# Expert rows loaded in blocks of 32 by 32 and turned by VectorE instead of TensorE

## The chip, the cores and the metric

The kernel runs on one core of one Trainium2 chip. The metric is device time in microseconds (us) of one launch; lower is better. Everything computes in f32 apart from routing masks and a few bf16 helpers.

## What is computed

The input has 32 sequences of 256 tokens with 128 channels (8192 tokens). There are two layers. Each normalises its input, computes an attention `s` and a mixture of experts `g`, and adds `s * silu(g)` to the input:

```python
xn = layernorm(x);  x = x + attention0(xn) * silu(moe0(xn))   # layer 0
xn = layernorm(x);  x = x + attention1(xn) * silu(moe1(xn))   # layer 1
# moe0: sigmoid gate, the best 2 of 8 experts, every token served; plus a shared expert
# moe1: softmax gate, the best 2 of 8 experts, at most 2048 places for each expert
# expert e: act(rows @ up_w[e] + up_b[e]) @ down_w[e] + down_b[e],  128 -> 512 -> 128
```

## The kernel before

The program is written out by hand for each engine, in the order in which the engine is to do things; semaphores order the engines among each other.

**Stages.** Routing decides for every token two places in a table of rows in HBM (`xd0`, `xd1`, one row of 132 floats for a place: 128 channels, and in word 128 the row of the result table to which the expert's output goes). POOL scatters the normalised rows there with indirect DMAs. When all are there, the experts run over **tiles** of 256 places: 71 tiles in layer 0 (`x0`) and 64 in layer 1 (`x1`). In layer 0 this stage stands between the first attention and the shared expert; in layer 1 it is put into the second attention, after its sequence 21.

**One tile.** In the text, tile i of a layer takes these steps:

- SP loads the 256 rows with one DMA into one of 6 buffers `X` (L453, two rows of 132 floats on each of 128 partitions). In layer 0, SP also loads each tile's expert weights: it reads the expert's number into a register (L437), then loads `up_w` (L438), `down_w` (L439) and the bias `down_b` (L441) into one of 5 buffers; layer 1 keeps an expert's weights for eight tiles and nearly all of them are loaded by ACT's queue.
- TensorE turns the two blocks of 128 rows with transposes into PSUM (`turn`, L1830), since the matmuls contract over channels and need them on the partitions.
- VectorE copies the turned rows to `XG` in SBUF (L1427), and computes the row numbers of the results, `to` (L1431).
- TensorE multiplies by `up_w` (`up`, L1839, four products of 256 columns), ScalarE applies bias and activation into `HH` (L874), and TensorE multiplies by `down_w` (`down`, L1848, 8 products).
- VectorE adds `down_b` (L1439, `result`), and POOL scatters the 256 result rows with two indirect DMAs (L622).

**Order.** TensorE goes turn(i+1), up(i), down(i-1), so a tile costs it the three steps. VectorE goes turned(i+1), result(i-1). SP goes, for each tile, rows of tile i+5, then the weights of tile i+4. Rows may be loaded into a buffer once `turn` and `to` of the tile before in it are done; weights once `edown` and `y` (down and result) of the tile before in their buffer are done:

```python
for i in range(x.n):                      # expert_rows, on SP
    if i + 5 < x.n:
        load(i + 5)
    if n == 0 and 1 <= i < x.n - 4:
        expert_weights(e, m, s, i + 4)
```

Tiles 0 to 3 of the rows and tiles 0 to 4 of the weights are loaded ahead of the stage. At its start in layer 0, SP waits for the end of the first attention (`yt`), loads constants and five blocks of the input (L528 to L532, L490), and then goes on with the rows of tile 4.

In layer 1 the first tiles stand around a piece of the second attention: TensorE does turn(0), up(0), then `output_second` of sequence 21, then turn(1) and turn(2).

Of the kernel before, what the change touches and what calls it, by code (L numbers as in the profile page):

```python
# [8 lines left out]
ALU = mybir.AluOpType  # L9
# [154 lines left out]
def memory(nc, ctx, a, out):  # L164
    m = Mem()

    def sbx(stack, name, shape, dt=F32):
        return stack.enter_context(nc.sbuf_tensor("s_" + name, shape, dt))
# [95 lines left out]
    es = ExitStack()  # L264
    m.DBt = [sbx(es, f"DBt{k}", [P, C]) for k in range(5)]
    x = m.x0 = Mem()
    x.n, x.base, x.NWB, x.NXB = NX0, 0, 5, 6
    x.W = [sbx(es, f"W0_{k}", [P, 2, 512]) for k in range(5)]
    x.X = [sbx(es, f"X0_{k}", [P, 2, ROW]) for k in range(6)]
    x.XG = [sbx(es, f"XG0_{k}", [P, SL]) for k in range(2)]  # L270
    x.HH = [sbx(es, f"HH0_{k}", [P, 4, SL]) for k in range(2)]
    x.Y = [sbx(es, f"Y0_{k}", [P, 2, C]) for k in range(4)]
    x.xr = m.xd0[0:NX0 * SL, :].rearrange("(i t p) c -> i p t c", p=P, t=2)
    x.yd = m.yd0
    m.H = [sbx(es, f"H{k}", [P, 4, 512]) for k in range(2)]
    m.swu = sbx(es, "swu", [P, HID])
# [37 lines left out]
    bt = ExitStack()  # L314
# [27 lines left out]
    x = m.x1 = Mem()  # L342
    x.n, x.base, x.NWB, x.NXB = NX1, NX0, 2, 6
    x.W = [sbx(bt, f"W1_{k}", [P, 2, 512]) for k in range(2)]
    x.X = [sbx(bt, f"X1_{k}", [P, 2, ROW]) for k in range(6)]
    m.b1s, m.b2s = sbx(bt, "b1s", [P, E, 4]), sbx(bt, "b2s", [P, E, C])
    bt.close()

# [15 lines left out]
    x = m.x1  # L364
    x.XG = [carve([SL]) for k in range(2)]
    x.HH = [carve([4, SL]) for k in range(2)]
    x.Y = [carve([2, C]) for k in range(4)]
    x.xr = m.xd1[0:NX1 * SL, :].rearrange("(i t p) c -> i p t c", p=P, t=2)
    x.yd = m.yd1
    carve = carver()  # L370
    m.ZG = [carve([8 * C]).rearrange("p (c k n) -> p c k n", c=4, k=2) for k in range(NF)]
# [6 lines left out]
def semaphores(nc, ctx):  # L378
    s = Sems()

    def sem(name):
        return ctx.enter_context(nc.semaphore(name))

    s.v_seq = sem("v_seq")

    s.const, s.upb, s.sw, s.zero, s.w0, s.c1, s.bb = (sem("l_" + n) for n in ("const", "upb", "sw", "zero", "w0", "c1", "bb"))
    s.zero_y, s.placed, s.to, s.nb, s.norm_a, s.norm_p, s.cnt_row = (sem(n) for n in (
        "l_zero_y", "placed", "to", "nb", "norm_a", "norm_p", "cnt_row"))

    s.wv0, s.vl, s.va, s.vd = (sem(n) for n in ("l_wv0", "vl", "va", "vd"))  # L390
    s.x = [sem(f"l_x{k}") for k in range(8)]
    s.scat0, s.scat1 = sem("l_scat0"), sem("l_scat1")

    s.zero_ready, s.var, s.rstd, s.norm, s.xpose, s.xt = (sem(n) for n in (
        "zero_ready", "var", "rstd", "norm", "xpose", "xt"))

    s.gate, s.gate_exp, s.onehot, s.cnt, s.cnt_sb, s.rank, s.total, s.total_sb, s.low, s.low_used, s.slots, s.ub = (
        sem(n) for n in ("gate", "gate_exp", "onehot", "cnt", "cnt_sb", "rank", "total", "total_sb", "low", "low_used",
                         "slots", "ub"))

    s.zvm, s.proj, s.rt, s.rq, s.ka, s.qm, s.vm, s.sc1, s.ev1, s.mask, s.sc2, s.prod, s.pv, s.yt = (sem(n) for n in (
        "zvm", "proj", "rt", "rq", "ka", "qm", "vm", "sc1", "ev1", "mask", "sc2", "prod", "pv", "yt"))

    s.turn, s.xg, s.eup, s.eact, s.edown, s.y = (sem(n) for n in ("turn", "xg", "eup", "eact", "edown", "y"))
    s.W = [[sem(f"l_W{n}_{k}") for k in range((5, 2)[n])] for n in range(2)]
    s.X = [[sem(f"l_X{n}_{k}") for k in range(6)] for n in range(2)]
    s.Y = [[sem(f"l_Y{n}_{k}") for k in range(4)] for n in range(2)]

    s.sup, s.hact, s.sdown = (sem(n) for n in ("sup", "hact", "sdown"))
    s.xb = [sem(f"l_xb{k}") for k in range(5)]  # L410
    s.yg = [sem(f"l_yg{k}") for k in range(3)]
    s.x1d = [sem(f"l_x1d{k}") for k in range(5)]
    s.comb, s.u, s.tanh, s.oproj, s.p6, s.x1, s.lg1, s.lg_sb = (sem(n) for n in (
        "comb", "u", "tanh", "oproj", "p6", "x1", "lg1", "lg_sb"))
# [30 lines left out]
def expert_rows(e, m, s, x, n):  # L445
    X, Y = s.X[n], s.Y[n]

    def load(i):
        k = i - x.NXB
        if k >= 0:  # L450
            e.wait_ge(s.turn, x.base + k + 1)
            e.wait_ge(s.to, x.base + k + 1)
        e.dma_start(x.X[i % x.NXB][:], x.xr[i]).then_inc(X[i % x.NXB], 16)  # L453

    for i in range(4):
        load(i)
# [8 lines left out]
    for k in range(4):  # L465
        e.wait_ge(Y[k], 32 * len(range(k, x.n, 4)))
# [952 lines left out]
def expert_dve(e, m, s, x, n, bias):  # L1419
    if n == 1:  # L1420
        e.wait_ge(s.bb, 32)

    def turned(i):
        e.wait_ge(s.turn, x.base + i + 1)
        if x.base + i >= 2:
            e.wait_ge(s.eup, 4 * (x.base + i - 1))
        e.tensor_copy(x.XG[i % 2][:], m.PS[6 + (i + n) % 2][:, 0:SL]).then_inc(s.xg, 1)  # L1427
        e.wait_ge(s.X[n][i % x.NXB], 16 * (i // x.NXB + 1))
        if i >= 8:
            e.wait_ge(s.Y[n][i % 4], 32 * (i // 4 - 1))  # L1430
# [12 lines left out]
    if n == 1:
        divide_second(e, m, s, MOE_AFTER)
        keep_second(e, m, s, MOE_AFTER)
    for i in range(x.n):
        if i + 1 < x.n:
            turned(i + 1)
        if i >= 1:
            result(i - 1)  # L1450
    if n == 1:
        maxima_dve(e, m, s, MOE_AFTER + 2, 0)
    result(x.n - 1)
# [360 lines left out]
def expert_pe(e, m, s, x, n):  # L1814
    PS = m.PS
# [6 lines left out]
        e.wait_ge(s.W[1][k % 2], 32 * (k // 2 + 1))  # L1822
        return x.W[k % 2]

    def turn(i):
        e.wait_ge(s.X[n][i % x.NXB], 16 * (i // x.NXB + 1))
        if x.base + i >= 2:
            e.wait_ge(s.xg, x.base + i - 1)
        for t in range(2):
            ins = e.transpose(PS[6 + (i + n) % 2][:, t * P:(t + 1) * P], x.X[i % x.NXB][:, t, 0:C], m.ident[:])  # L1830
        ins.then_inc(s.turn, 1)

    def up(i):
        W = weights(i)
        e.wait_ge(s.xg, x.base + i + 1)
        for j in range(4):
            if x.base + i >= 1:
                e.wait_ge(s.eact, 4 * (x.base + i - 1) + j + 1)
            e.matmul(PS[j][:, 0:SL], W[:, 0, j * P:(j + 1) * P], x.XG[i % 2][:], start=True, stop=True).then_inc(s.eup, 1)  # L1839
# [9 lines left out]
                               W[:, 1, j * C:(j + 1) * C], start=(j == 0), stop=(j == 3))  # L1849
        ins.then_inc(s.edown, 1)  # L1850

    turn(0)
    for i in range(x.n):
        if n == 1 and i == 0:
            up(0)
            output_second(e, m, s, MOE_AFTER)
            e.wait_ge(s.given, MOE_AFTER + 1)
            turn(1)
            continue
        if i + 1 < x.n:  # L1860
            turn(i + 1)
        up(i)
        if i >= 1:
            down(i - 1)
    if n == 1:
# [56 lines left out]
def tensor_program(e, m, s):  # L1922
    PS = m.PS
# [21 lines left out]
    for u in range(-1, NU + 4):  # L1945
        v, b = u % 6, u // 6
# [21 lines left out]
                route_ranks(e, m, s, m.r0, 0, stage - 2)  # L1968
        if v == 4 and b + 2 < NB:
            projection(e, m, s, b + 2, 0)  # L1970
    e.wait_ge(s.yt, NB)
    expert_pe(e, m, s, m.x0, 0)

    e.wait_ge(s.sw, 80)
    shared_up(e, m, s, 0)
    for g in range(NG):
# [25 lines left out]
    for t in range(NB + 1):  # L2002
# [42 lines left out]
        if t == MOE_AFTER:  # L2045
            weigh(e, m, s, t, 1)
            e.wait_ge(s.maxv, 4 * t + 8)
            e.wait_ge(s.ex, 4 * t + 4)
            e.wait_ge(s.mvt, t + 2)
            e.wait_ge(s.qs, t + 4)  # L2050
            expert_pe(e, m, s, m.x1, 1)


# [113 lines left out]
```

## Time and profile before

| | |
|---|---|
| median of 3 runs | 1727.6 us (1726.49 to 1728.92) |
| span of the profiled execution, first to last instruction | 1723.8 us |
| TensorE busy, share of the span | 95% |
| VectorE, ScalarE, POOL busy | 57%, 57%, 48% |
| mean granted TensorE clock | 0.994 of full speed |
| DMA traffic | 170.05 MB in 172423 packets, mean 99 GB/s |
| layer 0's experts on TensorE | from 527.15 to about 793.5 us |
| layer 1's experts on TensorE | from 1323.62 to about 1567 us |

No time of its own is given for the profiled execution beyond its span; the span is 3.8 us under the median of the runs, which takes in what lies around the first and the last instruction. Matmuls are pipelined, so their busy times overlap and the distance between starts tells what a step costs.

### The profile page before, as it was taken

The numbers are of one execution on the slowest core, as the hardware profiler recorded it, in microseconds if no ns is written. First come the engines' busy times: TensorE is split into PE (matmuls) and PEld (weight loads), VectorE is DVE, ScalarE is ACT, GpSimd is POOL, SyncE is SP. The second block draws the span as 40 slices with busy tenths as digits, with TensorE's granted clock in tenths as the row PEclk, the third lists the DMA queues.
The fourth block names the chain that finished last, engine by engine and source line by source line (L and its number), as shares of the span: only waits on it lengthen the run. The fifth ranks groups of instructions, "written<-read, shape, count | busy, mean of one in ns | idle before, by whom it ended". The sixth has DMA issues, their size and how long they took to land.

```text
span 1723.8 us, 49824 instructions
## 1 busy us (share of the span) xinstructions
PE 1629.9 (95%) x19349; PEld 1175.9 (68%) x19353; DVE 986.2 (57%) x2085; ACT 987.3 (57%) x2039; POOL 828.9 (48%) x906
## 2 busy tenths in 40 slices
PE   7999999999999999999998899898988999999995
PEld 5545454555547999998777566565656999997664
DVE  6788898777772222223999676454544222224887
ACT  5667666667664444444555465555555444445773
POOL 7343687877773454552122102555553555553323
PEclk9999999999999999999999899999999999999999
DMA  9900003000016777873342100111112223322434
GB/s 312 416 18 2 16 28 98 28 28 28 30 37 178 234 231 229 234 230 100 110 134 80 52 3 14 36 36 35 36 34 55 83 86 95 86 74 75 125 101 118
DMA packets 172423, 170.05 MB, mean 99 GB/s; under 512 B 20800, under 2 KB 139584, under 8 KB 169248
## 3 DMA queue, kind: packets, MB, share of 16 engines
q1 hardware_dynamic: 152768, 128.84, 24.9%
q0 software_dynamic: 16832, 34.64, 5.9%
q10 hardware_dynamic: 2592, 3.38, 0.7%
q8 instruction: 158, 2.59, 0.6%
q14 instruction: 73, 0.60, 0.1%
HBM read 97.16 MB, written 69.63 MB: 97 GB/s over the span
## 4 chain that ended last, share of the span: by engine, by line
PE 76%; DVE 7%; issue 5%; POOL 4%; another core or an unknown queue 3%; ACT 3%; DMA 1%; SPq 0%; POOLq 0%; DVEq 0%; ACTq 0%
PE ps L1848 14%; PE ps L1839 13%; PE ps L1641 10%; PE ps L1665 4%; PE ps L1605 4%; PE ps L1887 3%; PE ps L1875 3%; PE ps L1732 3%; PE ps L1798 3%; PE ps L1769 3%; PE ps L1606 2%; PE ps L1802 2%; PE ps L1779 2%; DVE s_RS L1318 2%
## 5 line engine op out<-in xcount | busy, mean ns | idle before, releaser
L605 POOL DMA_INDIRECT xd<-s_XN,s_slots x256 | 251.1, 981 | 143.8 <-issue 78.1
L793 ACT ACTIVATE s_S<-ps 128x512 f32<-128x512 f32 x384 | 209.9, 595 | 146.5 <-PE ps L1641 133.6
L1495 DVE TENSOR_TENSOR s_PP<-ps,s_S 128x1024 f32<-128x1024 f32 x192 | 234.4, 1221 | 85.4 <-PE ps L1641 52.8
L1641 PE MATMUL ps<-s_QM,s_KK 32*128 32x512 f32 x1536 | 241.6, 638 | 3.7 <-ACT s_S L793 3.6
L1318 DVE TENSOR_REDUCE s_RS<-ps 128x8 f32<-128x1024 f32 x128 | 150.7, 1218 | 160.6 <-PE ps L1736 85.3
L859 ACT ACTIVATE s_PX<-ps,s_scl 128x1024 f32<-128x1024 f32 x128 | 135.7, 1111 | 186.0 <-PE ps L1779 186.0
L622 POOL DMA_INDIRECT yd<-s_Y,s_to x142 | 136.1, 959 | 137.5 <-DVE s_to L1431 109.6
L874 ACT ACTIVATE s_HH<-ps,s_LG 128x256 f32<-128x256 f32 x284 | 123.6, 474 | 136.8 <-PE ps L1839 135.5
L638 POOL TENSOR_SCALAR_AFFINE_SELECT s_S<-s_S 128x1024 f32<-128x1024 f32 x128 | 140.7, 1099 | 120.8 <-ACT s_S L793 115.3
L874 ACT ACTIVATE s_XN<-ps,s_b1s 128x256 f32<-128x256 f32 x256 | 113.1, 474 | 126.3 <-PE ps L1839 120.2
L622 POOL DMA_INDIRECT yd<-s_XN,s_to x128 | 122.7, 958 | 129.8 <-DVE s_to L1431 102.6
L1439 DVE TENSOR_TENSOR s_Y<-ps,s_DBt 128x256 f32<-128x256 f32 x71 | 30.1, 425 | 199.5 <-PE ps L1848 188.3
L1848 PEld LDWEIGHTS ps<-s_W,s_HH 128*128 128x128 f32 x1136 | 137.8, 192 | 3.6
L1848 PE MATMUL ps<-s_W,s_HH 128*128 128x128 f32 x1136 | 138.1, 275 | 0.0
L1839 PE MATMUL ps<-s_XG,s_W 128*128 128x256 f32 x568 | 134.5, 380 | 0.9 <-DVE s_XG L1427 0.9
L1665 PEld LDWEIGHTS ps<-s_PP,s_VM 128*32 128x32 f32 x3072 | 76.3, 109 | 85.5 <-DVE s_PP L1495 50.5
L1439 DVE TENSOR_TENSOR s_XN<-ps,s_b2s 128x256 f32<-128x256 f32 x64 | 27.2, 425 | 183.9 <-issue 165.9
L1848 PEld LDWEIGHTS ps<-s_W,s_XN 128*128 128x128 f32 x1024 | 124.3, 192 | 3.3
L1848 PE MATMUL ps<-s_W,s_XN 128*128 128x128 f32 x1024 | 124.6, 275 | 0.0
L1839 PE MATMUL ps<-s_XN,s_W 128*128 128x256 f32 x512 | 121.3, 380 | 1.0 <-issue 1.0
L1798 PE MATMUL ps<-s_PX,s_VN 128*32 128x64 f32 x4096 | 98.8, 221 | 22.3 <-issue 13.9
L1641 PEld LDWEIGHTS ps<-s_QM,s_KK 32*128 32x128 f32 x1536 | 76.7, 182 | 63.3 <-issue 62.2
(224 smaller groups left out, 3009.5 us busy)
## 6 DMA issues: line engine op xcount, KB each, us to landing
s_W<-in_up_w SPq DMA_DIRECT2D x71, 256.0 KB
s_W<-in_down_w SPq DMA_DIRECT2D x71, 256.0 KB
s_X<-xd SPq DMA_DIRECT2D x135, 132.0 KB
xd<-s_zero SPq DMA_DIRECT2D x16, 1056.0 KB, 18.1
s_YG<-yd SPq DMA_DIRECT2D x32, 256.0 KB, 3.7
s_XN<-yd SPq DMA_DIRECT2D x32, 256.0 KB, 4.0
yd<-s_zero SPq DMA_DIRECT2D x7, 1056.0 KB, 27.9
s_DBt<-in_down_b SPq DMA_DIRECT2D x71, 64.0 KB
```

Source lines behind the costliest of these rows:

```text
L605: e.indirect_dma_start(out=xd, out_offset=bass.IndirectOffsetOnAxis(ap=m.slots[:, k, i:i + 1], axis=0), in_=m.XNp[:, i, 0:C + 1], in_offse ...
L622: e.indirect_dma_start(out=x.yd, out_offset=bass.IndirectOffsetOnAxis(ap=to[:, t:t + 1], axis=0), in_=x.Y[i % 4][:, t, :], in_offset=None) ...
L638: e.affine_select(out=sel, in_=sel, pattern=[[0, 8], [1, P]], compare_op=ALU.is_ge, fill=0.0, base=0, channel_multiplier=-1).then_inc(s.ma ...
L793: e.mul(m.S1[u % 3][:, t * 512:(t + 1) * 512], m.PA[:, t * 512:(t + 1) * 512], 1.0 / 64.0).then_inc(s.ev1, 1)
L874: e.activation(x.HH[i % 2][:, j, :], m.PS[j][:, 0:SL], func, bias=bias(i, j)).then_inc(s.eact, 1)
L1318: e.tensor_reduce(m.MM[b % 2][:, hf, 8 * rp:8 * rp + 8], m.ps[:, 1024 * rp:1024 * rp + 1024].rearrange("p (x n) -> p x n", x=8), AX.X, ALU ...
L1495: e.tensor_tensor(m.PP[u % 4][:], m.PB[u % 2], m.S1[u % 3][:], ALU.mult).then_inc(s.prod, 1)
L1641: return e.matmul(out, m.KK[k][32 * r:32 * r + 32, kind, kc * P:(kc + 1) * P], m.QM[k][32 * r:32 * r + 32, kind, :, qc * P:(qc + 1) * P], ...
L1665: i = e.matmul(m.PS[6][32 * c:32 * c + 32, qc * P:(qc + 1) * P], m.VM[b % 2][:, kc, 4 * c + h, :], m.PP[(2 * q + c // 2) % 4][:, (c % 2) * ...
L1798: e.matmul(P4[32 * c:32 * c + 32, qb * 64:qb * 64 + 64], m.VN[b % 2][:, qb, 4 * c + hh, :], PX[:, c, x * 256 + qb * 64:x * 256 + qb * 64 + ...
L1839: e.matmul(PS[j][:, 0:SL], W[:, 0, j * P:(j + 1) * P], x.XG[i % 2][:], start=True, stop=True).then_inc(s.eup, 1)
L1848: ins = e.matmul(PS[4 + i % 2][:, c * P:(c + 1) * P], x.HH[i % 2][:, j, c * P:(c + 1) * P], W[:, 1, j * C:(j + 1) * C], start=(j == 0), st ...
```

## The change

SP loads a tile of rows with five DMAs instead of one. Four of them each load 32 channels of all 256 rows: partition 32q+p gets, for each of 8 groups of 32 rows, the 32 channels 32q to 32q+31 of row p of the group. So every block of 32 rows by 32 channels lies as a block of 32 partitions by 32 words, and the four quarters of the channels stand on the four quarters of the partitions. The fifth loads words 128 to 131 of each row. VectorE's transpose turns every block of 32 by 32 in place of the copy from PSUM, and its output is `XG` as before. TensorE's `turn`, its PSUM use and the semaphore `turn` are gone. A buffer of rows is free once `xg` and `to` are done. Rows count as loaded at 80 instead of 16 on their semaphore. TensorE's wait for `yt` stands after the experts of layer 0 instead of before; two waits ahead of layer 1's experts and one in them are gone, since the PSUM banks of the turned rows are no longer used.

```diff
+ROW_LOADS = 5 * 16
...
-    x.X = [sbx(es, f"X0_{k}", [P, 2, ROW]) for k in range(6)]
+    x.X = [sbx(es, f"X0_{k}", [P, 2 * ROW]) for k in range(6)]
...
     def load(i):
         k = i - x.NXB
         if k >= 0:
-            e.wait_ge(s.turn, x.base + k + 1)
+            e.wait_ge(s.xg, x.base + k + 1)
             e.wait_ge(s.to, x.base + k + 1)
-        e.dma_start(x.X[i % x.NXB][:], x.xr[i]).then_inc(X[i % x.NXB], 16)
+        rows, to, loaded = x.rows[i * SL:(i + 1) * SL, :], x.X[i % x.NXB], X[i % x.NXB]
+        for q in range(4):
+            e.dma_start(to[32 * q:32 * q + 32, 0:SL].rearrange("p (b c) -> p b c", c=32),
+                        rows[:, 32 * q:32 * q + 32].rearrange("(b p) c -> p b c", p=32)).then_inc(loaded, 16)
+        e.dma_start(to[:, SL:2 * ROW].rearrange("p (t c) -> p t c", t=2), rows[:, C:ROW].rearrange("(t p) c -> p t c", p=P)
+                    ).then_inc(loaded, 16)
...
     def turned(i):
-        e.wait_ge(s.turn, x.base + i + 1)
+        X = x.X[i % x.NXB]
+        e.wait_ge(s.X[n][i % x.NXB], ROW_LOADS * (i // x.NXB + 1))
         if x.base + i >= 2:
             e.wait_ge(s.eup, 4 * (x.base + i - 1))
-        e.tensor_copy(x.XG[i % 2][:], m.PS[6 + (i + n) % 2][:, 0:SL]).then_inc(s.xg, 1)
-        e.wait_ge(s.X[n][i % x.NXB], 16 * (i // x.NXB + 1))
+        e.transpose(x.XG[i % 2][:], X[:, 0:SL]).then_inc(s.xg, 1)
...
-    def turn(i):
-        e.wait_ge(s.X[n][i % x.NXB], 16 * (i // x.NXB + 1))
-        if x.base + i >= 2:
-            e.wait_ge(s.xg, x.base + i - 1)
-        for t in range(2):
-            ins = e.transpose(PS[6 + (i + n) % 2][:, t * P:(t + 1) * P], x.X[i % x.NXB][:, t, 0:C], m.ident[:])
-        ins.then_inc(s.turn, 1)
-
...
-    turn(0)
     for i in range(x.n):
+        up(i)
         if n == 1 and i == 0:
-            up(0)
             output_second(e, m, s, MOE_AFTER)
-            e.wait_ge(s.given, MOE_AFTER + 1)
-            turn(1)
-            continue
-        if i + 1 < x.n:
-            turn(i + 1)
-        up(i)
         if i >= 1:
             down(i - 1)
...
+    expert_pe(e, m, s, m.x0, 0)
+
     e.wait_ge(s.yt, NB)
-    expert_pe(e, m, s, m.x0, 0)
-
...
             e.wait_ge(s.ex, 4 * t + 4)
-            e.wait_ge(s.mvt, t + 2)
-            e.wait_ge(s.qs, t + 4)
             expert_pe(e, m, s, m.x1, 1)
```

SP, in the middle of layer 0's experts: what it issues for one tile. `TENSOR_LOAD` and `ISA` read the expert's number and make addresses; `s_W_k` are buffers of weights, `s_X_k` of rows; the column at the end of a row lists the semaphores that it waits for. Before:

```order
L437 TENSOR_LOAD s_LG [waits y,edown]
L437 ISA x2
L438 ISA
L438 DMA s_W_3<-in_up_w 128x512
L439 DMA s_W_3<-in_down_w 128x512
L441 ISA
L441 DMA s_DBt<-in_down_b 128x128
L453 DMA s_X_4<-xd 128x2x132 [waits to,turn]
```

Changed:

```order
L438 TENSOR_LOAD s_LG [waits y,edown]
L438 ISA x2
L439 ISA
L439 DMA s_W_3<-in_up_w 128x512
L440 DMA s_W_3<-in_down_w 128x512
L442 ISA
L442 DMA s_DBt<-in_down_b 128x128
L456 DMA s_X_4<-xd 32x8x32 [waits to,xg]
L456 DMA s_X_4<-xd 32x8x32 x3
L458 DMA s_X_4<-xd 128x2x4
```

SP issues eight DMAs for a tile instead of four, in the same place of its order.

TensorE, in the same place: two tiles' worth of its order. `s_HH` are the activations, `s_XG` the turned rows. Before:

```order
L1848 MATMUL ps<-s_W_2,s_HH_0 128x128 [waits y,eact,l_W0_2]
L1848 MATMUL ps<-s_W_2,s_HH_0 128x128 x7
L1830 MATMUL ps<-s_ident,s_X_5 128x128 [waits xg,l_X0_5]
L1830 MATMUL ps<-s_ident,s_X_5 128x128
L1839 MATMUL ps<-s_XG_0,s_W_4 128x256 [waits eact,xg,l_W0_4]
L1839 MATMUL ps<-s_XG_0,s_W_4 128x256 [waits eact] x3
L1848 MATMUL ps<-s_W_3,s_HH_1 128x128 [waits y,eact,l_W0_3]
L1848 MATMUL ps<-s_W_3,s_HH_1 128x128 x7
```

Changed:

```order
L1846 MATMUL ps<-s_W_3,s_HH_1 128x128 [waits y,eact,l_W0_3]
L1846 MATMUL ps<-s_W_3,s_HH_1 128x128 x7
L1837 MATMUL ps<-s_XG_1,s_W_0 128x256 [waits eact,xg,l_W0_0]
L1837 MATMUL ps<-s_XG_1,s_W_0 128x256 [waits eact] x3
L1846 MATMUL ps<-s_W_4,s_HH_0 128x128 [waits y,eact,l_W0_4]
L1846 MATMUL ps<-s_W_4,s_HH_0 128x128 x7
```

The two transposes of a tile are gone, and `up` follows `down` directly.

## Rows read from the trace of the kernel before

**Rows 1.** Two stretches inside the experts, layer 0 and layer 1, by engine; last columns PEclk, DMA share, GB/s.
```profile
600.00:700.00 100.00, 100.00 (x700) 94.51 (x700) 23.33 (x81) 46.55 (x108) 51.19 (x54) 1.00 0.80 232
1350.00:1500.00 150.00, 150.00 (x1049) 141.75 (x1048) 32.98 (x120) 70.95 (x161) 77.19 (x81) 1.00 0.32 91
```

**Rows 2.** Timeline of TensorE, last tiles of layer 0: start us, us, engine, line, operation.
```profile
784.47 0.38 PE L1830 MATMUL ps<-s_ident,s_X 128*128 128x128 f32 x2
784.69 1.89 PE L1839 MATMUL ps<-s_XG,s_W 128*128 128x256 f32 x8
786.42 1.95 PE L1848 MATMUL ps<-s_W,s_HH 128*128 128x128 f32 x16
788.20 1.89 PE L1839 MATMUL ps<-s_XG,s_W 128*128 128x256 f32 x8
789.93 3.73 PE L1848 MATMUL ps<-s_W,s_HH 128*128 128x128 f32 x32
793.50 1.02 PE L1875 MATMUL ps<-s_XT,s_swu 128*128 128x512 f32 x2
```

**Rows 3.** Timeline of SP's queue, where layer 0's experts begin.
```profile
527.12 0.35 SPq L528 DMA_DIRECT2D s_swu<-in_sw_up  x1
527.52 0.43 SPq L529 DMA_DIRECT2D s_swd<-in_sw_down  x1
...
528.94 0.44 SPq L532 DMA_DIRECT2D s_WO<-in_wout  x1
...
532.65 1.73 SPq L453 DMA_DIRECT2D s_X<-xd  x3
```

**Rows 4.** Timeline of SP's queue, weights of tiles 0, 1 and 2 loaded ahead.
```profile
274.25 0.36 SPq L438 DMA_DIRECT2D s_W<-in_up_w  x1
274.72 0.37 SPq L439 DMA_DIRECT2D s_W<-in_down_w  x1
275.27 0.33 SPq L441 DMA_DIRECT2D s_DBt<-in_down_b  x1
276.38 0.34 SPq L438 DMA_DIRECT2D s_W<-in_up_w  x1
...
278.47 0.34 SPq L438 DMA_DIRECT2D s_W<-in_up_w  x1
```

**Rows 5.** Waits of SP's queue from 540 to 790 us: total, times, longest.
```profile
SPq L436 <- DVE s_Y L1439: 42.6, 37, 1.9
```

**Rows 6.** Instructions on the row buffers: duration ns min/median/max, first and last start.
```profile
L453 SPq DMA_DIRECT2D s_X<-xd x135: 4/382/707, 509.4 to 1535.2; - x135
```

**Rows 7.** DMA queues from 510.5 to 513.5 us, while four tiles of rows are loaded.
```profile
q1 hardware_dynamic: 1083, 0.54, 76.5%
```

**Rows 8.** DMA queues from 973.5 to 974 us, while `b1` is loaded in pieces of 16 bytes.
```profile
DMA packets 681, 0.04 MB, mean 70 GB/s; under 512 B 675, under 2 KB 675, under 8 KB 681
q1 hardware_dynamic: 681, 0.04, 105.3%
```

**Rows 9.** DMA issues of the whole run: size, and median us from issue to landing.
```profile
s_swu<-in_sw_up SPq DMA_DIRECT2D x1, 256.0 KB, 2.7
```

**Rows 10.** Groups of lines from 500 to 900 us: xcount, busy us, mean ns, idle before.
```profile
L622 POOL DMA_INDIRECT yd<-s_Y,s_to x142 | 136.1, 959 | 137.5 <-DVE s_to L1431 109.6 <-issue 21.6 <-DVE s_Y L1439 6.3
L1427 DVE COPY s_XG<-ps 128x256 f32<-128x256 f32 x71 | 29.6, 417 | 8.4 <-PE ps L1830 5.3 <-PE ps L1839 2.5
```

**Rows 11.** Timeline of all engines, where layer 1's experts begin.
```profile
1320.65 17.17 SPq L453 DMA_DIRECT2D s_X<-xd  x11
...
1324.15 0.42 DVE L1427 COPY s_XN<-ps 128x256 f32<-128x256 f32 x1 [5.86 <-PE ps L1830]
...
1324.56 1.75 DVE L1340 RECIPROCAL s_RC<-ps 128x256 f32<-128x256 f32 x1
...
1332.85 1.89 PE L1839 MATMUL ps<-s_XN,s_W 128*128 128x256 f32 x8
...
1336.58 1.89 PE L1839 MATMUL ps<-s_XN,s_W 128*128 128x256 f32 x8
```

More of the change, by code:

```diff
@@ L272, in memory @@
     x.Y = [sbx(es, f"Y0_{k}", [P, 2, C]) for k in range(4)]
-    x.xr = m.xd0[0:NX0 * SL, :].rearrange("(i t p) c -> i p t c", p=P, t=2)
+    x.rows = m.xd0[0:NX0 * SL, :]
     x.yd = m.yd0
@@ L344, in memory @@
     x.W = [sbx(bt, f"W1_{k}", [P, 2, 512]) for k in range(2)]
-    x.X = [sbx(bt, f"X1_{k}", [P, 2, ROW]) for k in range(6)]
+    x.X = [sbx(bt, f"X1_{k}", [P, 2 * ROW]) for k in range(6)]
     m.b1s, m.b2s = sbx(bt, "b1s", [P, E, 4]), sbx(bt, "b2s", [P, E, C])
@@ L367, in memory @@
     x.Y = [carve([2, C]) for k in range(4)]
-    x.xr = m.xd1[0:NX1 * SL, :].rearrange("(i t p) c -> i p t c", p=P, t=2)
+    x.rows = m.xd1[0:NX1 * SL, :]
     x.yd = m.yd1
@@ L402, in semaphores @@
         "zvm", "proj", "rt", "rq", "ka", "qm", "vm", "sc1", "ev1", "mask", "sc2", "prod", "pv", "yt"))
-    s.turn, s.xg, s.eup, s.eact, s.edown, s.y = (sem(n) for n in ("turn", "xg", "eup", "eact", "edown", "y"))
+    s.xg, s.eup, s.eact, s.edown, s.y = (sem(n) for n in ("xg", "eup", "eact", "edown", "y"))
     s.W = [[sem(f"l_W{n}_{k}") for k in range((5, 2)[n])] for n in range(2)]
@@ L1423, in turned @@
     def turned(i):
-        e.wait_ge(s.turn, x.base + i + 1)
+        X = x.X[i % x.NXB]
+        e.wait_ge(s.X[n][i % x.NXB], ROW_LOADS * (i // x.NXB + 1))
         if x.base + i >= 2:
             e.wait_ge(s.eup, 4 * (x.base + i - 1))
-        e.tensor_copy(x.XG[i % 2][:], m.PS[6 + (i + n) % 2][:, 0:SL]).then_inc(s.xg, 1)
-        e.wait_ge(s.X[n][i % x.NXB], 16 * (i // x.NXB + 1))
+        e.transpose(x.XG[i % 2][:], X[:, 0:SL]).then_inc(s.xg, 1)
         if i >= 8:
             e.wait_ge(s.Y[n][i % 4], 32 * (i // 4 - 1))
-        e.tensor_tensor(m.to[i % 8][:], x.X[i % x.NXB][:, :, C], m.row[:, 2 * i:2 * i + 2], ALU.max).then_inc(s.to, 1)
+        e.tensor_tensor(m.to[i % 8][:], X[:, SL:2 * ROW].rearrange("p (t c) -> p t c", t=2)[:, :, 0], m.row[:, 2 * i:2 * i + 2], ALU.max).then_inc(s.to, 1)
     def result(i):
```

## The prediction

> **What bounds the kernel now.** I read first the busy times in two stretches inside the experts [rows 1]: TensorE is busy all the time in both, VectorE a quarter of it, the DMA engines 80% in layer 0 and 32% in layer 1, and the granted clock is 1.00, the 2.4 GHz level. So a tile costs what TensorE's three steps cost. The timeline shows this distance [rows 2]: `down` starts 1.73 us after `up` (784.69 to 786.42); the next `up` starts 1.78 us after `down` where no transposes stand between (786.42 to 788.20), and where they do, they add 0.22 us (784.47 to 784.69). So a tile takes 1.73 + 1.78 + 0.22 = 3.73 us before, as in layer 1 [rows 11] (1332.85 to 1336.58), and would take 3.51 us without them.
>
> Then I read SP's queue, since the change gives it four more DMAs for each tile. DMAs issued back to back start 0.40 us apart the first time and 0.473 us after it (527.52 to 528.94 are three distances, over loads of 2 KB to 256 KB) [rows 3]; I take 0.475. A tile's weights, without any wait, take 2.10 us (276.38 to 278.47, and 2.13 before it), of which 1.35 are the three DMAs' and the rest reads the expert's number [rows 4]. So SP needs 2.10 + 0.475 = 2.58 us of the 3.73 us of a tile in layer 0, and waits some 1.1 us in each. The waits show part of it: 42.6 us in 37 tiles for `y` alone [rows 5].
>
> **The change, part by part.**
>
> *TensorE's transposes go.* 0.22 us for each of 71 and 64 tiles, if nothing else decides. Some 61 tiles of layer 1 stand in the regular loop: 61 x 0.22 = 13.4 us.
>
> *VectorE's transpose takes the place of the copy* (0.417 us [rows 10]). The trace shows no such transpose. Below, it could cost half the copy; above, 1.75 us, the dearest operation of 256 columns here [rows 11], a reciprocal. With 1.75 VectorE would be busy 23.33 / 26.9 + 1.33 = 2.2 us in each tile, under 3.51, and the buffer `XG` is written one whole `up`, `down` ahead of its use. So it costs nothing at either end; I take 0.4 us. Nothing is queued behind it that TensorE needs sooner: the bias addition behind it is needed by the `down` after the next. POOL needs 2 x 0.96 + 0.3 = 2.2 us of each tile [rows 10], so it doesn't bind at 3.51 either.
>
> *SP issues five DMAs for the rows.* In layer 0: 2.10 + 5 x 0.475 = **4.48 us** for each tile, against 3.51 us of TensorE. This covers nothing any more: SP becomes the bound, and TensorE waits for weights in each tile. The price of one issue is bounded from both sides: single issues of this line took from 4 to 707 ns, half of them 382 or more [rows 6]; three behind the queue's busiest moment took 1.73 us, so 0.58 each [rows 3]. With 0.38 a tile takes 4.0 us, with 0.58 it takes 5.0. I take 0.475, the nearest row of back-to-back issues.
>
> *The DMA engines get 1280 pieces for a tile instead of 256* (1024 of 128 bytes, 256 of 16). Four old loads: 1083 packets, mostly of 528 bytes, in 0.765 x 3 us x 16 engines, so 34 ns each [rows 7]. Pieces of 16 bytes: 681 in 1.053 x 0.5 x 16, so 12.4 ns [rows 8]. A piece of 128 bytes lies between; by its bytes I take 17 ns, nearer the 16 bytes. A tile of layer 0 now uses 0.80 x 100 x 16 / 26.9 = 47.6 us of engine time (700 matmul records at 26 for a tile are 26.9 tiles [rows 1]). It loses 256 x 34 ns = 8.7, gains 256 x 12.4 ns = 3.2 and 1024 pieces at 12.4 to 34 ns, 12.7 to 34.8. That is 55 to 77 us over 16 engines: 3.4 to 4.8 us for a tile, 3.7 at 17 ns. So they stay under SP's 4.48, if not by much. In layer 1 a tile uses 0.32 x 3.73 x 16 = 19 us, then 26 to 49 us, 1.6 to 3.0 us over the engines: under 3.51.
>
> SP's part is where a rule of the notes speaks against my sum. The Trainium skill (DMA: Bandwidth & Descriptors, "Issuing engines are not separate DMA queues") says that the sequencer's time for starting a DMA is usually small next to the DMA itself. By it SP would not count, and TensorE would bind at 3.51 us; the issue distances and SP's 1.1 us of room say otherwise here.
>
> *Sum for layer 0.* SP is free for the rows of tile 4 at 532.65 as before [rows 3]. Rows of tiles 4, 5 and 6: 15 x 0.475 = 7.1 us, 539.8. The weights of tile 5 start 0.7 us later, at 540.5 (the gap of 276.38 behind 275.27 + 0.33 [rows 4]). Then 64 tiles at 4.48 to those of tile 69: 827.2; tile 70 has no rows with it: 829.3. Its last DMA is issued 1.0 us later and lands 2.7 us after [rows 9]: 833.0. From its `up` to the end of the stage are 793.50 - 788.20 = 5.3 us [rows 2]: 838.3 against 793.5, **+44.8 us**. The start without the wait for `yt` and two turns gives TensorE 1.5 us, and by 545 it has caught up with SP, so they are worth nothing.
>
> *Sum for layer 1.* -13.4 us. At its start SP is late, not TensorE: the rows' load begins at 1320.65, when the scatters are in [rows 11]. The fifth DMA is issued 1.9 us later, lands near 1325.3, and VectorE's turn ends at 1325.7 instead of 1324.6; the reciprocal behind it (1324.56) is that much later, and the attention's output after it. The turn of tiles 1 and 2 on TensorE is saved. Together **+1 us**. After that SP needs 2.4 us for each tile and gains on TensorE.
>
> Total: +44.8 - 13.4 + 1 = **+32.4 us**. The profiled span 1723.8 becomes 1756; the runs' median stands 3.8 us higher, so 1727.6 + 32.4 = **1760 us**.
>
> **The rivals.**
>
> 1. *SP's issues fit into its room, and TensorE binds at 3.51 us (faster).* This is what happens if an issue costs under (3.51 - 2.10) / 5 = 0.28 us. The time: 71 x 0.22 + 1.5 + 13.4 - 1 = 29.5 us less, 1698 us. For it: single issues as short as 4 ns [rows 6]. Against: not one pair of neighbours is closer than 0.40 us [rows 3, 4]. 6%.
>
> 2. *The DMA engines bind (slower still).* If pieces of 128 bytes cost more than (4.48 x 16 - 42.1) / 1024 = 29 ns. At twice a 528-byte piece, 68 ns, a tile of layer 0 takes (42.1 + 69.6) / 16 = 7.0 us and one of layer 1 (13.6 + 69.6) / 16 = 5.2: 66 x 3.27 = 216 and 61 x 1.47 = 90 us more, 2034 us. At 45 ns they take 5.5 and 3.7 us, layer 1's gain is gone too, and 1727.6 + 66 x 1.8 gives 1846 us. For it: shares of 80% before anything is added, and SP's issues stretch to 0.58 when the engines are full. Against: the 12.4 ns of a 16-byte piece. 15%. The Trainium skill (DMA: Bandwidth & Descriptors, "Specifications") asks for at least 512 bytes and says that smaller ones are read, modified and written; if that doubled them, the 2034 us would follow.
>
> 3. *Nearly hidden.* At 0.38 us for an issue [rows 6], 4.0 us for a tile: 65 x (4.48 - 4.0) = 31 us less than the forecast, 1729 us: no change. For it, the median of single issues; against, that back-to-back ones lie wider. 4%.
>
> **How the numbers follow.** My forecast, SP as the bound at 4.3 to 5.0 us for a tile, has 75%: 1760 - 65 x 0.18 = 1748 to 1760 + 65 x 0.52 = 1794. The upper end takes in engines at 4.8 us too. With some of rival 2 above it the range is 1745 to 1805. A measurement of this kernel tells about 0.2% (3.5 us) from no change. Faster by more: rival 1 and part of 3, 7%; within: 3%; slower: 90%.
>
> **What would show it.** In the changed profile, SP's queue in layer 0's experts is a solid row of issues from 533 to 830 us, eight in each 4.5 us, with no wait for `y` or `to`; TensorE's `up` waits for a weights' DMA, and its busy share falls to 3.51 / 4.48 = 78%; the experts end near 838 us. DMA share 0.8 to 0.9 there. In layer 1 `up` starts every 3.51 us, TensorE never idle. VectorE's transposes near 0.4 us, and no one waits for them. I am wrong if SP waits in layer 0 while TensorE is full (rival 1), or if SP's issues stretch and the DMA share is at 1 (rival 2).

## The result, and the profile after

The changed kernel takes 1790.8 us (median of 4 runs, 1786.2 to 1793.5), the kernel before 1727.05 beside it: 1.0371 times as long, with a 95% interval of 1.0348 to 1.0393. It is slower by 63.7 us, inside the range given (1745 to 1805), but twice the +32.4 us forecast. The profiled execution took 1786.2 us, with a span of 1784.5.

The same stretch of layer 0 as in [rows 1], one around it, and one of layer 1 (columns as there):

```profile
600.00:700.00 100.00, 81.12 (x499) 72.98 (x498) 16.95 (x62) 35.59 (x82) 38.40 (x40) 0.96 0.69 178
540.00:840.00 300.00, 237.28 (x1479) 212.68 (x1478) 50.76 (x186) 108.62 (x246) 119.56 (x125) 0.98 0.69 176
1450.00:1600.00 150.00, 150.00 (x1028) 141.21 (x1027) 34.38 (x126) 71.16 (x170) 81.81 (x86) 1.00 0.48 95
```

In layer 0 TensorE went from 100% to 79% busy, and no other engine, nor the DMA engines at 0.69, filled up. Layer 1 stays full. The chain of waits, followed back from the last instruction, names who took the time. Its shares by engine, before and then after:

```profile
PE 76%; DVE 7%; issue 5%; POOL 4%; another core or an unknown queue 3%; ACT 3%; DMA 1%; SPq 0%; POOLq 0%; DVEq 0%; ACTq 0%
PE 63%; SPq 11%; issue 8%; DVE 6%; POOL 4%; DMA 3%; ACT 3%; another core or an unknown queue 3%; POOLq 0%; DVEq 0%; ACTq 0%
```

SPq is SP's queue: 11% of 1784.5 is 196 us in which the end hung on SP issuing DMAs. The waits from 520 to 860 us, TensorE's and then all that SP had from 540 to 850:

```profile
PE ps L1837 <- DMA s_DBt<-in_down_b: 66.8, 57, 3.1
```
```profile
SPq L438 <- PE ps L1846: 0.3, 1, 0.3
```

TensorE waits in 57 tiles for the last DMA of the weights, and SP, which waited 42.6 us for `y` alone before [rows 5], waits once. Its queue, for two tiles (start us, duration us, line, operation):

```profile
596.90 1.87 SPq L456 DMA_DIRECT2D s_X<-xd  x4
598.81 0.45 SPq L458 DMA_DIRECT2D s_X<-xd  x1
600.07 0.36 SPq L439 DMA_DIRECT2D s_W<-in_up_w  x1
600.53 0.38 SPq L440 DMA_DIRECT2D s_W<-in_down_w  x1
601.09 0.33 SPq L442 DMA_DIRECT2D s_DBt<-in_down_b  x1
601.52 1.86 SPq L456 DMA_DIRECT2D s_X<-xd  x4
...
606.12 1.86 SPq L456 DMA_DIRECT2D s_X<-xd  x4
```

A regular tile costs 4.61 us (596.90 to 601.52 to 606.12), of which the first is made up of 1.91 for the four loads of blocks, then 1.26 for the words and the reading of the next expert's number (598.81 to 600.07), then 1.45 for the weights (600.07 to 601.52).

But the mean of the 64 distances from the weights of tile 5 (541.31) to those of tile 69 (853.04) is 4.87, and their median 4.66. Some tiles look like this:

```profile
570.39 0.38 SPq L440 DMA_DIRECT2D s_W<-in_down_w  x1
570.95 1.21 SPq L442 DMA_DIRECT2D s_DBt<-in_down_b  x1
572.26 0.38 SPq L456 DMA_DIRECT2D s_X<-xd  x1
```
```profile
q1 hardware_dynamic: 290, 0.01, 19.7%
q8 instruction: 1, 0.02, 6.7%
```
```profile
590.18 1.47 SPq L440 DMA_DIRECT2D s_W<-in_down_w  x1
```

The first fence is SP's queue; the 64-KB bias takes 1.21 us to issue instead of 0.33. The second lists the DMA queues from 570 to 570.9 us: one packet of 16 KB on the queue named `instruction`, which I read as code that an engine fetches, besides the pieces of the rows. The third is the next such place. Of the 64 distances 12 hold such a fetch, and these are 0.9 us longer in the mean (5.61 instead of 4.70); they make 11.3 of the 13.3 us by which all 64 exceed their median.

The end of layer 0 on TensorE, to be read against [rows 2]; then layer 0's block transposes on VectorE and layer 1's `up` on TensorE (duration ns min/median/max, first and last start):

```profile
857.73 1.99 PE L1837 MATMUL ps<-s_XG,s_W 128*128 128x256 f32 x8 [1.15 <-DMA s_DBt<-in_down_b]
...
866.64 0.59 PE L1866 MATMUL ps<-s_XT,s_swu 128*128 128x512 f32 x1
```
```profile
L1434 DVE STREAM_TRANSPOSE s_XG<-s_X x71: 433/435/446, 525.4 to 857.0; 128x256 f32<-128x256 f32 x71
L1837 PE MATMUL ps<-s_XN,s_W x512: 379/379/454, 1398.5 to 1621.5; 128*128 128x256 f32 x171
```

So the difference of the spans, 60.7 us, is: layer 0's experts end at 866.64 instead of 793.50, **+73.1**; from there to layer 1's first `up` 531.9 instead of 531.2, +0.7; layer 1 from its first `up` to its last 223.0 (second line of the fence) instead of 237.1, **-14.1**; the tail +1.0.

### The profile page after: what moved, and what is told of

Its sections match the earlier page's. It is cut to its first block, busy times and chain, and to the rows that moved or that the text cites. A ratio compares the mean times of both kernels' runs of the same rounds, so it can differ in the third digit from the quotient of the medians.

```text
span 1784.5 us, 49571 instructions
## 1 busy us (share of the span) xinstructions
PE 1624.7 (91%) x19079; PEld 1157.2 (65%) x19083; DVE 984.6 (55%) x2085; ACT 984.1 (55%) x2039; POOL 830.3 (47%) x906
## 4 chain that ended last, share of the span: by engine, by line
PE 63%; SPq 11%; issue 8%; DVE 6%; POOL 4%; DMA 3%; ACT 3%; another core or an unknown queue 3%; POOLq 0%; DVEq 0%; ACTq 0%
PE ps L1647 9%; PE ps L1837 8%; PE ps L1846 8%; SPq L456 4%; PE ps L1671 4%; PE ps L1611 3%; PE ps L1878 3%; PE ps L1738 3%; PE ps L1866 3%; PE ps L1804 3%; PE ps L1775 3%; PE ps L1612 2%; PE ps L1808 2%; DMA s_DBt<-in_down_b 2%
## 5 line engine op out<-in xcount | busy, mean ns | idle before, releaser
L1837 PE MATMUL ps<-s_XG,s_W 128*128 128x256 f32 x568 | 146.5, 403 | 66.9 <-DMA s_DBt<-in_down_b 66.8
L880 ACT ACTIVATE s_XN<-ps,s_b1s 128x256 f32<-128x256 f32 x256 | 107.7, 475 | 118.2 <-PE ps L1837 86.1
L1837 PEld LDWEIGHTS ps<-s_XG,s_W 128*128 128x128 f32 x568 | 105.8, 196 | 90.9 <-DMA s_DBt<-in_down_b 77.9
```

The source lines that it names most:

```text
L880: e.activation(x.HH[i % 2][:, j, :], m.PS[j][:, 0:SL], func, bias=bias(i, j)).then_inc(s.eact, 1)
```

## The experiments

The theory: SP's queue binds in layer 0 by the number of its issues. Its rivals: the small pieces (their time on the DMA engines, or their making), VectorE's transpose, and the fetches of code. l1_only, one_dma, whole_rows and pairs ran beside a kernel before of 1726.2 us; split_five, act_issues, split_three and short_down beside one of 1726.0. three_by_rows, pairs_rows and act_pairs ran on a chip where the kernel before took 1675.3 us, so of those only the ratio to the kernel before and the distance are compared with the others. "Distance" is the mean distance from one tile's weight loads to the next one's on SP, over the same 64 tiles of layer 0 in each trace; it is 4.87 after the change, and 3.73 before it, where TensorE sets it.

**l1_only: the change in layer 1 alone.**

```diff
+        if n == 0:
+            e.dma_start(x.X[i % x.NXB][:].rearrange("p (t c) -> p t c", t=2),
+                        x.rows[i * SL:(i + 1) * SL, :].rearrange("(t p) c -> p t c", p=P)).then_inc(X[i % x.NXB], 16)
+            return
...
+    if n == 0:
+        e.wait_ge(s.yt, NB)
+        turn(0)
```

> The change in layer 1 alone; layer 0 loads whole rows and turns them on TensorE as before. If SP's issues in layer 0 are the whole loss and layer 1 is a clean gain of 0.22 us for each of its tiles, the time is 13 to 15 us under the kernel before, about 1713 us, and a tile of layer 0 takes 3.73 us again. If the change also costs something outside layer 0 (small pieces in layer 1's DMAs, VectorE), it is nearer to 1727 us.

1714.1 us, 0.9939 of before [0.9917, 0.9962]: 12.1 us faster, a little less than the 13 to 15 expected. Layer 0's stretch is again that of [rows 1], so all of the loss stood there:

```profile
600.00:700.00 100.00, 100.00 (x700) 94.48 (x699) 23.06 (x81) 46.53 (x107) 50.75 (x54) 1.00 0.78 230
```

**one_dma: the same 1024 pieces of 128 bytes for each tile, issued by one DMA instead of four** (which channels land where is shuffled, so the output is another).

```diff
-        for q in range(4):
-            e.dma_start(to[32 * q:32 * q + 32, 0:SL].rearrange("p (b c) -> p b c", c=32),
-                        rows[:, 32 * q:32 * q + 32].rearrange("(b p) c -> p b c", p=32)).then_inc(loaded, 16)
+        e.dma_start(to[:, 0:SL].rearrange("p (b c) -> p b c", c=32),
+                    rows.rearrange("(p t) (k c) -> p (t k) c", t=2, c=33)[:, :, 0:32]).then_inc(loaded, 16)
```

> The same 1024 pieces of 128 bytes and 256 of 16 bytes for each tile, but in two DMAs instead of five: one loads all the pieces of 128 bytes. It takes its 32 words from other places of the rows, so the experts get shuffled channels; all else is computed. SP theory: SP needs 4.62 - 3 x 0.475 = 3.2 us for a tile of layer 0, TensorE binds at 3.51 us, and the time falls to 1697 to 1705 us. Engine theory (the small pieces are what costs, in the DMA engines or in making them): a tile stays above 4.4 us and the time near 1780 us. In between: engines at 3.7 to 4.2 us for a tile, 1710 to 1750 us.

1716.1 us, 0.9947 [0.9931, 0.9964]; distance 3.79 instead of 4.87. With as many pieces and three issues fewer, the loss is gone. But the time is 11 us above the 1697 to 1705 that the theory asked for. The stretch:

```profile
545.00:790.00 245.00, 233.62 (x1556) 216.22 (x1557) 52.79 (x194) 110.74 (x260) 124.16 (x130) 1.00 0.89 227
```

TensorE is busy 95%. It isn't full, and SP, which waited for other engines 4.0 us in these 245, is still the bound: the issue behind the 1024 pieces takes 0.65 us where it takes 0.45 after the change, a first sign that many pieces hold the queue up.

```profile
643.15 0.53 SPq L455 DMA_DIRECT2D s_X<-xd  x1
643.74 0.65 SPq L457 DMA_DIRECT2D s_X<-xd  x1
```

**whole_rows: five DMAs as in the change, but in pieces of 512 bytes** (a quarter as many; what stands in the blocks is other data).

```diff
-            e.dma_start(to[32 * q:32 * q + 32, 0:SL].rearrange("p (b c) -> p b c", c=32),
-                        rows[:, 32 * q:32 * q + 32].rearrange("(b p) c -> p b c", p=32)).then_inc(loaded, 16)
+            e.dma_start(to[32 * q:32 * q + 32, 0:SL].rearrange("p (t c) -> p t c", c=C),
+                        rows[64 * q:64 * q + 64, 0:C].rearrange("(t p) c -> p t c", p=32)).then_inc(loaded, 16)
```

> Five DMAs for each tile as in the changed kernel, but the four large ones load 64 whole rows each, in pieces of 512 bytes (256 instead of 1024 pieces). The rows are not laid out for the turn, so the experts get shuffled data; all else is computed. SP theory: no change against the changed kernel, 4.6 to 4.85 us for a tile of layer 0, 1776 to 1791 us; the lower end if the stalls of about 1.1 us in some of SP's issues come from the number of pieces. Engine theory: it falls towards TensorE's 3.51 us, 1700 us.

1783.7 us, 1.0327 [1.0306, 1.0348]; distance 4.81, a regular tile 4.52. It lies in the range of the SP theory. Of the 64 us of loss at most some 7 come from the size of the pieces. The places of 1 us at a fetch stay (+1.1 us each), so they don't come from small pieces either.

**split_five: the kernel before, its one load of rows in layer 0 split into five** (four quarters of 32 partitions, and the words). TensorE still turns the rows, VectorE still copies, no piece of 128 bytes.

```diff
-        e.dma_start(x.X[i % x.NXB][:], x.xr[i]).then_inc(X[i % x.NXB], 16)
+        for q in range(4):
+            e.dma_start(to[32 * q:32 * q + 32, :, 0:C], x.xr[i][32 * q:32 * q + 32, :, 0:C]).then_inc(loaded, 16)
+        e.dma_start(to[:, :, C:ROW], x.xr[i][:, :, C:ROW]).then_inc(loaded, 16)
```

> The kernel before, with layer 0's rows loaded by five DMAs (four quarters of the partitions, in pieces of 512 bytes, and the words), the turns on TensorE as before. SP theory: a tile of layer 0 takes 4.8 us as in the changed kernel, although nothing is turned by VectorE and no piece of 128 bytes is loaded: about 70 us over the kernel before, 1795 us. Engine theory: under 10 us over it.

1795.2 us, 1.0402 [1.0384, 1.0419], +69, as expected: the split alone brings nearly the whole loss of layer 0 (+73.1). A regular tile takes 4.51 us (604.25 to 608.76), the mean is 4.76:

```profile
604.25 0.36 SPq L438 DMA_DIRECT2D s_W<-in_up_w  x1
...
605.70 1.79 SPq L458 DMA_DIRECT2D s_X<-xd  x4
607.53 0.43 SPq L459 DMA_DIRECT2D s_X<-xd  x1
608.76 0.46 SPq L438 DMA_DIRECT2D s_W<-in_up_w  x1
```

**act_issues: the changed kernel whole, but in layer 0 three of the four block loads are issued on ScalarE's queue**, behind its four activations of a tile.

```diff
-        for q in range(4):
+        for q in range(1 if n == 0 and i >= 6 else 4):
...
+        if n == 0 and 1 <= i and i + 5 < x.n:
+            e.wait_ge(s.xg, i)
+            rows, to = x.rows[(i + 5) * SL:(i + 6) * SL, :], x.X[(i + 5) % x.NXB]
+            for q in range(1, 4):
+                e.dma_start(to[32 * q:32 * q + 32, 0:SL].rearrange("p (b c) -> p b c", c=32),
+                            rows[:, 32 * q:32 * q + 32].rearrange("(b p) c -> p b c", p=32)).then_inc(s.X[0][(i + 5) % x.NXB], 16)
```

> The changed kernel, with three of the four quarter loads of layer 0 issued by ACT's queue behind the activations of a tile, and SP's share down to one quarter and the words; the same pieces in the same DMAs, nothing left out. If SP's queue is what binds (its own time for an issue), SP needs 3.2 us and ACT 1.8 + 1.4 = 3.2 us for a tile, and the time falls to 1700 to 1715 us. If what binds is shared by both queues (making 1280 descriptors, or the engines), it falls by less than 20 us from 1790.

1709.4 us, 0.9908 [0.9892, 0.9925]; distance 3.58. The same DMAs with the same pieces; only the queue that issues them is another, and 81 us are back, as the SP theory expected (1700 to 1715):

```profile
600.00:700.00 100.00, 98.49 (x671) 92.33 (x670) 22.37 (x83) 46.13 (x111) 53.59 (x56) 1.00 0.92 241
```

This is the strongest evidence for the bound, and against the DMA engines (0.92, with TensorE busy 98%) and the transpose.

**split_three: the kernel before, three loads in layer 0** (two halves of 64 partitions, and the words).

```diff
+        for q in range(2):
+            e.dma_start(to[64 * q:64 * q + 64, :, 0:C], x.xr[i][64 * q:64 * q + 64, :, 0:C]).then_inc(loaded, 16)
+        e.dma_start(to[:, :, C:ROW], x.xr[i][:, :, C:ROW]).then_inc(loaded, 16)
```

> The kernel before, with layer 0's rows loaded by three DMAs instead of one (two halves of the partitions, in pieces of 512 bytes, and words 128 to 131 of each row), the turns on TensorE as before. SP needs 4.62 - 2 x 0.475 = 3.67 us for a tile in its regular distance, and 3.85 with stalls of 0.2 us a tile, against TensorE's 3.73. SP theory: 5 to 12 us over the kernel before. Engine theory (small pieces, not issues): no change, within 3 us.

1764.7 us, 1.021 [1.0186, 1.0234]: +39, where 5 to 12 was expected: a miss. Distance 4.31, and (4.31 - 3.73) x 64 = 37 us. Each of these three issues took 0.60 us:

```profile
569.58 1.24 SPq L458 DMA_DIRECT2D s_X<-xd  x2
570.87 0.59 SPq L459 DMA_DIRECT2D s_X<-xd  x1
```

**three_by_rows: the same, but the halves are taken by rows**, so that each covers all 128 partitions in half as many pieces on each.

```diff
-            e.dma_start(to[64 * q:64 * q + 64, :, 0:C], x.xr[i][64 * q:64 * q + 64, :, 0:C]).then_inc(loaded, 16)
+            e.dma_start(to[:, q, 0:C], x.xr[i][:, q, 0:C]).then_inc(loaded, 16)
```

> As split_three, but the two large DMAs take one row of each of 128 partitions instead of both rows of 64 partitions. In split_three every one of the three issues took 0.60 us, where one for 32 or for 128 partitions took 0.45 to 0.475 elsewhere. If the 64 partitions are the reason, a tile takes 3.9 us or less and the time is 1730 to 1740 us; if not, 4.3 us and 1765 us.

1676.3 us, 1.0007 [0.9997, 1.0018]: nothing lost, even a little better than expected (1730 to 1740 us, or 1.002 to 1.008). Distance 3.80. As many issues, bytes and pieces, but some 0.43 us each:

```profile
557.69 0.85 SPq L458 DMA_DIRECT2D s_X<-xd  x2
558.59 0.43 SPq L459 DMA_DIRECT2D s_X<-xd  x1
```

So the price of an issue depends on how the DMAs are shaped, and halves of 64 partitions are the dear shape here. The third DMA, the words, is the same in both kernels and is dearer too (0.59 against 0.43), so the price isn't a matter of the single DMA's own shape alone. Nothing points to the other chip as the reason: loads of 32 partitions cost the same on both (0.46 us from start to start in whole_rows and in pairs_rows, below). Why the 64 partitions are dear, no run tells.

**pairs: the rows of two tiles in the same five DMAs**, in both layers, three buffers of two tiles each; nothing is left out.

```diff
-    x.X = [sbx(es, f"X0_{k}", [P, 2 * ROW]) for k in range(6)]
+    x.X = [sbx(es, f"X0_{k}", [P, 4 * ROW]) for k in range(3)]
...
-            e.dma_start(to[32 * q:32 * q + 32, 0:SL].rearrange("p (b c) -> p b c", c=32),
+            e.dma_start(to[32 * q:32 * q + 32, 0:c * SL].rearrange("p (b c) -> p b c", c=32),
```

> As the changed kernel, with the rows of two tiles loaded by the same five DMAs (16 blocks for a partition instead of 8), in three buffers of two tiles; nothing is left out. SP needs (2 x 2.2 + 2.4) / 2 = 3.4 us for a tile of layer 0. SP theory: TensorE binds at 3.51 us, or SP just above it with its stalls (3.65 us); 1697 to 1710 us. Engine theory: as the changed kernel, 1780 to 1790 us.

1739.9 us, 1.0092 [1.007, 1.0114]; distance 4.09. It wins 51 us back, but stays 30 us above the 1697 to 1710 that SP's count promised: a miss. The issues themselves grew, the one behind the four most:

```profile
622.63 2.02 SPq L456 DMA_DIRECT2D s_X<-xd  x4
624.70 1.13 SPq L458 DMA_DIRECT2D s_X<-xd  x1
626.68 0.31 SPq L439 DMA_DIRECT2D s_W<-in_up_w  x1
```

**pairs_rows: pairs, in pieces of 512 bytes** (512 of them instead of 2048; other data in the blocks), to tell whether that stretching comes from the pieces.

```diff
-            e.dma_start(to[32 * q:32 * q + 32, 0:c * SL].rearrange("p (b c) -> p b c", c=32),
-                        rows[:, 32 * q:32 * q + 32].rearrange("(b p) c -> p b c", p=32)).then_inc(loaded, 16)
+            e.dma_start(to[32 * q:32 * q + 32, 0:c * SL].rearrange("p (t c) -> p t c", c=C),
+                        rows[64 * c * q:64 * c * (q + 1), 0:C].rearrange("(t p) c -> p t c", p=32)).then_inc(loaded, 16)
```

> The rows of two tiles in five DMAs, as in the run of pairs, but the four large ones load whole rows, in pieces of 512 bytes (512 instead of 2048 pieces for two tiles). The rows are not laid out for the turn, so the experts get shuffled data; all else is computed. In pairs the DMA behind the four large ones took 1.2 us to issue instead of 0.45 and a tile 4.09 us. If SP is held up there by the making of so many pieces, that goes with them: a tile takes 3.5 to 3.6 us and the time falls from 1740 to 1700 to 1706 us. If it is the DMAs' size or the fetches, it stays at 1730 to 1740.

1655.2 us, 0.9883 [0.9866, 0.9899]; distance 3.63; expected were 3.5 to 3.6 and, as a ratio, 0.985 to 0.988. The stretching is gone (0.43 instead of 1.13):

```profile
564.58 1.81 SPq L456 DMA_DIRECT2D s_X<-xd  x4
566.44 0.43 SPq L458 DMA_DIRECT2D s_X<-xd  x1
```

So the queue has two prices here: so much for each DMA, and, where the pieces of one are many, so much for each piece. The load of the DMA engines isn't the difference: their share from 545 to 760 us is 0.81 in both runs. Whether the time goes into making the pieces or into passing them on isn't told. In pairs five DMAs with 2560 pieces held the queue for 3.20 us (622.63 to 625.83), so at most 1.25 ns a piece, if all of that time went to the pieces.

**act_pairs: pairs, and three of its four large loads on ScalarE's queue in layer 0**, nothing left out.

```diff
-        for q in range(4):
+        for q in range(1 if n == 0 and j >= 3 else 4):
...
+        if n == 0 and i % 2 == 1 and i + 5 < x.n:
+            e.wait_ge(s.xg, i + 1)
```

> As pairs, with three of the four large DMAs of layer 0 issued by ACT's queue; nothing is left out. SP then needs (2 x 2.2 + 1.0) / 2 = 2.7 us for a tile, ACT 1.8 + 0.8 = 2.6. If only SP's queue binds, TensorE does at 3.51 us: 1698 to 1703 us. If making the pieces holds up all queues, the tile stays at 3.55 us or more as in the run in which ACT issues for single tiles, and the time at 1705 to 1715 us.

1651.1 us, 0.9866 [0.9848, 0.9884], 24.2 us faster than the kernel before on that chip: the best version, and in the expected range (1698 to 1703 us, or 0.984 to 0.987). TensorE is full, at 3.51 us a tile (703.56 to 707.07):

```profile
545.00:760.00 215.00, 215.00 (x1472) 202.39 (x1471) 49.95 (x184) 107.37 (x244) 117.37 (x123) 1.00 0.96 247
```
```profile
703.56 1.89 PE L1845 MATMUL ps<-s_XG,s_W 128*128 128x256 f32 x8
705.29 1.95 PE L1854 MATMUL ps<-s_W,s_HH 128*128 128x128 f32 x16
707.07 1.89 PE L1845 MATMUL ps<-s_XG,s_W 128*128 128x256 f32 x8
```

The DMA share of 0.96 says that there is little left on the DMA engines.

**short_down: the changed kernel, with 2 of the 8 products of each `down` in layer 0** (6 are left out), to have fewer instructions on TensorE and so fewer fetches.

```diff
+                if n == 0 and j > 0:
+                    continue
```

> The changed kernel with three quarters of layer 0's second products left out (2 instead of 8 for a tile), so that TensorE has some 14 instead of 26 product records a tile to fetch and do; SP's work is the same. SP theory: TensorE's work in layer 0 is covered, so the distance of tiles stays at 4.6 us and more, and only the stage's end is shorter by some 3 us. If SP's stalls of 1 us come with the fetches of TensorE's instructions (they stand together in four traces), there are about half as many and the average distance falls from 4.84 to 4.73 us: 7 us more, 1780 us together. If the stalls have another cause, the distance stays at 4.84.

1781.0 us, 1.0317 [1.0299, 1.0334]; distance 4.81; 1780 us was expected. TensorE has 12 records a tile instead of 24 (the expectation said 14 instead of 26). Of the 64 distances 7 hold a fetch instead of 12, each still 0.8 us longer in the mean, and the mean distance fell by 0.06 us (4.87 to 4.81). Five places of 0.9 us fewer would give 0.07, so this agrees with the fetches as the cause, though the 4.73 expected is not reached, and 4 us between two traces is little to go by. In the kernels where SP binds, tiles with a fetch are longer by 0.2 us (split_three) to 1.1 us (whole_rows), in the kernel before by 0.2; that the fetch itself is what holds SP up is not shown.

## Why the prediction was right and where it was not

- **SP's queue becomes the bound in layer 0.** Right. SP has one wait left in 310 us, TensorE is busy 79% (78% was said), split_five makes the loss without any other part of the change, act_issues removes it by moving three issues.
- **4.48 us for a tile.** This is the step that failed: the mechanism held, but the term was mis-sized and measured 4.87. First, the median tile took 4.66: the five issues took 2.40 (2.375 was said), but weights and reading took 2.26 (1.45 + 0.81), not 2.10. The trace before showed weights only with no rows between them, and so without the 0.10 us from the end of the bias's issue to the start of the rows' (601.42 to 601.52). 64 x 0.18 makes 11.5 us. Second, the 13.3 us by which the longer tiles exceed the median, most of them tiles with a fetch: no term held them, since before the change SP's room of 1.1 us a tile swallowed such places. The start (+0.8), the last distance (+0.5) and the way from the last weights to the end (11.0 us instead of 9.0) add 3.3. These are the 28 us between +44.8 and +73.1.
- **The range.** That 1790.8 lies inside it is in part luck. Its upper part was made for issues of 0.58 us or for DMA engines at 4.8 us a tile; neither came. It was filled by the stalls at the fetches and by the steps between the loads, which the sum did not hold.
- **0.475 us for an issue.** Right for this shape (1.91 for four). It isn't one price: 0.60 in split_three, 1.13 behind many pieces in pairs. The bounds of 0.38 and 0.58 would have failed there.
- **The DMA engines don't bind.** Right. An estimate of the price of a piece of 128 bytes: 0.69 x 4.87 us x 16 = 53.8 us of engine time for a tile, less 42.1 without the blocks, over 1024 is 11 ns (one_dma: 11.6; layer 1: 13). I took 17, from bounds of 12.4 to 34. So the share stayed at 0.69, under the 0.8 to 0.9 said.
- **VectorE's transpose.** 0.435 us (0.4 was said) and no cost: TensorE waited for it once, 1.2 us, at the start of layer 1's experts.
- **TensorE's transposes.** 0.22 us for each tile of layer 1: -14.1 (said -13.4), and +0.7 at its start (said +1). l1_only gives it alone: -12.1.
- **The rivals.** Rival 1 asked for issues under 0.28 us; they took 0.48. But its time would have been 1698: act_pairs, which meets its condition in another way, wins 24 us against the 29.5 that it named. Rival 2 fell with the 11 ns, and act_issues and act_pairs carry the same pieces at shares of 0.92 and 0.96 without loss. Rival 3 asked for 4.0 us a tile.
- **The two rules of the Trainium skill** (DMA: Bandwidth & Descriptors). "Issuing engines are not separate DMA queues" calls the sequencer's time usually small beside the DMA. The trace doesn't agree for loads of 32 KB: five issues held SP for 2.40 of the 3.51 us that TensorE wants for a tile, 0.48 each, while the 256 pieces of one load are an estimated 256 x 11 ns / 16 = 0.18 us of all 16 DMA engines. "Specifications" warns of pieces under 512 bytes; here a piece of 128 bytes took the DMA engines an estimated 11 ns where one of mostly 528 bytes took 34 [rows 7], so for loads of this kind no doubling is seen.

Open is why tiles with a fetch are up to 1.1 us longer on SP, and why DMAs over 64 partitions are issued more slowly. Not tried: all five loads on ScalarE's queue, and act_pairs on a chip where the kernel before takes 1726 us.

## What to carry to other kernels

Before a load is split, add up all that its queue does for one turn of the loop, the reading of registers too, from one full turn as it will be, and set it against the distance that the bounding engine keeps: here 2.6 us of 3.73 left room for two more issues, not for four. A split that overruns the room can be saved by issuing on a queue whose engine has time (act_issues: 0.9908 of before). One DMA for two turns helps too, but by itself it didn't save this one (pairs: 1.0092), since its pieces were many; both together did best (act_pairs: 0.9866). Where the room is there, as in layer 1, the split costs nothing. And a queue without room shows every small stall that the room hid, so leave some in the sum.

## What was unexpected of the hardware

- From start to start, loads issued back to back stood 0.48 us apart over 32 partitions (596.90 to 598.81), 0.45 over 128 (557.69 to 558.59 in three_by_rows) and 0.64 over 64 (569.58 to 570.87 in split_three).
- Many small pieces hold up the issue behind them: 0.45 us behind four DMAs of 256 pieces, 0.65 behind one of 1024, 1.13 behind four of 512. At the estimate of at most 1.25 ns a piece, from pairs, 256 pieces take 0.32 us and fit between issues 0.48 us apart, 512 take 0.64 and don't.
- By the estimate above a piece of 128 bytes costs the DMA engines 11 ns, about the price of one of 16 bytes (12.4) and a third of that of one of 528 bytes (34).
- In short_down, with TensorE busy 67% in short bursts, its granted clock was 0.81 in the mean, between its levels of 1.2 and 2.4 GHz. In the same stretch it was 0.96 after the change, at 81% busy, and 1.00 in whole_rows, at 79%. No time hung on it in this stretch, since SP was the bound:

```profile
600.00:700.00 100.00, 66.58 (x245) 53.80 (x246) 17.16 (x63) 36.92 (x82) 41.23 (x43) 0.81 0.70 178
```

- On the chip of three_by_rows, pairs_rows and act_pairs the kernel before takes 1675.3 us instead of 1726. In three_by_rows, which takes the same time there, layer 1 has the 237.1 us from its first `up` to its last of the kernel before, while from layer 0's last `up` to layer 1's first there are 491.7 us instead of 535.0: most of the 51 us lie between the experts' stages. Why wasn't looked into.
